# Chunked gated linear attention with experts on one core: level products split by rows per head

## The reference

```python
x = x + layernorm(attn(layernorm(x)));  x = x + layernorm(ffn(layernorm(x)))
# attn, 4 heads, key size 64, value size 128, per batch and head:
q = (x @ Wq) * 64 ** -0.5;  k = x @ Wk;  v = x @ Wv
g = log_sigmoid(x @ gk_w1 @ gk_w2 + gk_b) / 16
for t in range(512):                       # S is 64 x 128
    S = exp(g[t])[:, None] * S + k[t][:, None] * v[t][None, :]
    o[t] = q[t] @ S
o = rms_norm(o) * rms_w * silu(x @ Wg);  out = o @ Wo
# ffn: the 16 x 512 tokens in 8 groups of 1024, one expert each: gelu(t @ w1 + b1) @ w2 + b2
```

## Time and profile before

| | |
|---|---|
| median of 3 runs | 1318.27 us (1318.04 to 1319.22) |
| profiled execution | 1316.67 us |
| its span | 1314.9 us, granted clock 0.988 |
| busy: PE / its weight loads / DVE / ACT / POOL | 95 / 83 / 79 / 54 / 48% of the span |
| instructions | 23430 |
| read from and written to HBM | 28.38 and 8.39 MB |

### The profile page before, as it was taken

How to read it: one execution, slowest core, us unless ns; L and a number is a source line. 1 busy time by engine, 2 the same in 40 slices (tenths; PEclk the granted TensorE clock), 3 DMA queues, 4 the chain that set the end, 5 groups by cost and what they waited for, 6 DMA issues and landing times. The chain is left out here.

```text
span 1314.9 us, 23430 instructions
## 1 busy us (share of the span) xinstructions
PE 1245.6 (95%) x8388; PEld 1096.4 (83%) x8388; DVE 1035.5 (79%) x2404; ACT 711.3 (54%) x1427; POOL 637.5 (48%) x889
## 2 busy tenths in 40 slices
PE   5889999999999999999999999999999999999957
PEld 3778889888898888889888888988889888898956
DVE  4769788796978969788787978879787796978863
ACT  5365555655456465654756555565545646465423
POOL 5436453563445544564435644356354554456431
PEclk9989999999999999999999999999999999999988
DMA  2110010100101001010011001010010100100000
GB/s 97 37 33 17 17 49 1 53 17 17 49 21 48 3 17 49 22 49 2 17 49 53 16 17 47 3 53 16 17 49 18 44 9 17 49 21 33 1 17 16
DMA packets 31778, 38.27 MB, mean 29 GB/s; under 512 B 2448, under 2 KB 29104, under 8 KB 31664
## 3 DMA queue, kind: packets, MB, share of 16 engines
q1 hardware_dynamic: 31136, 36.25, 8.3%
q10 hardware_dynamic: 528, 0.52, 0.1%
HBM read 28.38 MB, written 8.39 MB: 28 GB/s over the span
## 5 line engine op out<-in xcount | busy, mean ns | idle before, releaser
L1041 POOL TENSOR_TENSOR k_decayed<-k_decayed,block_totals 128x256 f32<-128x256 f32 x192 | 170.4, 887 | 248.3 <-PE ps_level L304 248.0
L304 PE MATMUL ps_level<-q_blockdiag,k_decayed 128*128 128x128 f32 x1792 | 263.9, 282 | 13.2 <-DVE q_blockdiag L586 12.5
L304 PEld LDWEIGHTS ps_level<-q_blockdiag,k_decayed 128*128 128x128 f32 x1792 | 234.9, 191 | 34.9 <-DVE q_blockdiag L586 24.6
L576 DVE COPY_PREDICATED attn_T<-level_masks,ps_level 128x512 f32<-128x512 uint32 x160 | 153.1, 957 | 21.6 <-PE ps_level L304 21.4
L1047 POOL TENSOR_TENSOR rstd<-rstd,minus_half 128x1 f32<-128x1 f32 x192 | 111.7, 584 | 106.5 <-DVE rstd L638 106.5
L586 DVE TENSOR_TENSOR q_blockdiag<-q_blockdiag,block_totals 128x512 f32<-128x512 f32 x192 | 140.0, 730 | 27.3 <-PE ps_level L304 27.2
L261 PE MATMUL ps_big<-w_ff_hi,h_hi 128*128 128x256 f32 x512 | 150.0, 293 | 2.5 <-DVE h_lo L591 2.5
L263 PE MATMUL ps_big<-w_ff_hi,h_lo 128*128 128x256 f32 x512 | 144.8, 283 | 0.0
L262 PE MATMUL ps_big<-w_ff_lo,h_hi 128*128 128x256 f32 x512 | 144.7, 283 | 0.0
L838 ACT ACTIVATE gelu_out<-ps_big,ff_b_cols 128x512 f32<-128x512 f32 x128 | 88.0, 688 | 80.2 <-PE ps_big L263 48.9
L624 DVE SCALAR_TENSOR_TENSOR o<-o,o_rstd,out_gate 128x128 f32<-128x128 f32 x256 | 93.3, 425 | 45.0 <-POOL o_rstd L1063 45.0
(11 more groups left out here) (110 smaller groups left out, 3203.1 us busy)
## 6 DMA issues: line engine op xcount, KB each, us to landing
w_raw<-L_ffn_w SPq DMA_DIRECT2D x16, 1024.0 KB, 5.5
out<-y SPq DMA_DIRECT2D x16, 512.0 KB, 2.9
x_in<-L_attn_x SPq DMA_DIRECT2D x15, 512.0 KB, 3.9
ff_b_rows<-L_ffn_b SPq DMA_DIRECT2D x8, 128.0 KB, 2.1
x_in<-L_attn_x ACTq DMA_DIRECT2D x1, 512.0 KB, 4.0
w_raw<-L_attn_Wv SPq DMA_DIRECT2D x1, 512.0 KB, 5.4
w_raw<-L_attn_Wg SPq DMA_DIRECT2D x1, 512.0 KB, 6.7
y<-L_attn_Wo SPq DMA_DIRECT2D x1, 512.0 KB, 7.7
```

The source lines that it names most:

```text
L304: last = nc.tensor.matmul(PL[tl][:, c * CH:(c + 1) * CH], kk[:, tl, c * CH:(c + 1) * CH], q[:, :, :, 1, :], start=True, stop=True)
L576: nc.vector.copy_predicated(dst, m.to_broadcast([P, 2 * NCH, HC // h, h]), src)\
L1041: nc.gpsimd.tensor_tensor(k, k, t.to_broadcast([P, T // (2 * h), h]), ALU.mult)\
```

## The change

- q is stored plainly in `q_decayed` (`qd`), 128 partitions by 512 tokens for each tile, written by DVE straight from PSUM. `q_blocks` on ACT falls. `q_update` handles half the elements, and stands ahead of the copy in DVE's queue.
- `level` takes each head alone: weights and streamed q are on 64 partitions, 64 columns are streamed, and the two heads write to two different banks. Even levels use `ps_out` and `ps_state`, odd ones `PL`, and a bank holds one head of both tiles. In the last level only the first 64 k tokens of a chunk are loaded. A level waits for the copies of the level before the last.
- The copies to attn_T go by head and not by tile, each after both tiles' products, one step later than before.
- `S` becomes block-diagonal, `state_blockdiag`. `state(c)` writes four pieces of 64 partitions; `att` multiplies plain q of a tile by 256 columns of S, two products for a chunk in place of four.
- The own-token products: `diag_rows` streams q times k over a 32-column indicator, chunk c on columns 32c to 32c+31 of the array, ahead of level 0; ACT copies the rows to a spare piece of `o`, and `diag_columns` transposes them.
- The transposes of k for the last chunk, which nothing uses, fall, and the last k update leaves that chunk out.

```diff
 def level(i, tl):
     ...
-                        if i - 1 < MASKED:
-                            pe.wait_ge(sem["dv_cp"], at("dv_cp", s, 2 * (i - 1) + tl + 1))
-                        else:
-                            pe.wait_ge(sem["ac_cp"], at("ac_cp", s, 2 * tl + 2))
+                        if i >= 2:
+                            pe.wait_ge(sem["dv_cp"], at("dv_cp", s, 2 * (i - 1)))
+                        elif C:
+                            pe.wait_ge(sem["dv_t"], at("dv_t", p, NCH))
+                    m = CH if i < NL - 1 else HC
                     for c in range(NCH):
-                        q = qbd[:, tl, :, c * CH:(c + 1) * CH].rearrange("p a (n t h) -> p a n t h", t=2, h=h)
-                        last = nc.tensor.matmul(PL[tl][:, c * CH:(c + 1) * CH],
-                                                kk[:, tl, c * CH:(c + 1) * CH], q[:, :, :, 1, :],
-                                                start=True, stop=True)
-                        if i == 0:
-                            self_product = diag(c, tl)
+                        for hh in range(2):
+                            r = slice(hh * HK, (hh + 1) * HK)
+                            q = qd[r, tl, c * CH:(c + 1) * CH].rearrange("p (n t h) -> p n t h", t=2, h=h)
+                            w = (tl * NCH + c) * HC
+                            last = nc.tensor.matmul(LVB[i % 2][hh][0:m, w:w + HC], kk[r, tl, c * CH:c * CH + m],
+                                                    q[:, :, 1, :], start=True, stop=True)
                     last.then_inc(sem["pe_lv"], 1)
+                def diag_rows():
     ...
+                    for tl in range(KT):
+                        for c in range(NCH):
+                            last = nc.tensor.matmul(PT[0][32 * c:32 * (c + 1), 0:CH], ind[:, tl, :],
+                                                    qk[:, tl, c * CH:(c + 1) * CH], start=(tl == 0), stop=(tl == KT - 1))
+                    last.then_inc(sem["pe_drow"], 1)
+
+                def diag_columns():
+                    pe.wait_ge(sem["ac_dg"], at("ac_dg", s, 1))
     ...
+                    nc.tensor.transpose(PT[1][:, 0:CH], o[:, 0, 0:CH], ident[:, :]).then_inc(sem["pe_diag"], 1)
 def att(c):
     ...
-                        if c:
-                            last = nc.tensor.matmul(PO[:, w], qbd[:, tl, hh, c * CH:(c + 1) * CH],
-                                                    S[:, tl, :], start=False, stop=True)
+                    if c:
+                        for tl in range(KT):
+                            last = nc.tensor.matmul(PO[:, tl * 2 * HV:(tl + 1) * 2 * HV], qd[:, tl, c * CH:(c + 1) * CH],
+                                                    S[:, tl, :], start=False, stop=(tl == KT - 1))
 queue of PE
+                        if step == 0:
+                            diag_rows()
                         level(step // 2, step % 2)
+                        if step == 1:
+                            diag_columns()
 queue of DVE
-                        if step // 2 < MASKED:
-                            copy_pairs(step // 2, step % 2)
                         q_update(step // 2, step % 2)
+                        if step == 1:
     ...
+                        if 1 <= step <= 2 * MASKED:
+                            copy_pairs((step - 1) // 2, (step - 1) % 2)
 def state(c): (DVE)
     ...
+                    for tl in range(KT):
+                        for hh in range(2):
+                            r = slice(hh * HK, (hh + 1) * HK)
+                            new, old = PS[r, tl * HV:(tl + 1) * HV], S[r, tl, hh * HV:(hh + 1) * HV]
     ...
 queue of ACT
-                def q_blocks(tl):
     ...
+                if B:
+                    act.wait_ge(sem["pe_drow"], at("pe_drow", s, 1))
+                    copy(o[:, 0, 0:CH], PT[0][:, 0:CH], "ac_dg")
```

More of the change, by code:

```diff
@@ L64, in build @@
         y = sb("y", [P, NCH, D])
-        qbd = sb("q_blockdiag", [P, KT, 2, T])
+        qd = sb("q_decayed", [P, KT, T])
         kk = sb("k_decayed", [P, KT, T])
@@ L72, in build @@
         kT = sb("k_tokens", [P, NCH, D])
-        S = sb("state", [P, KT, HV])
+        S = sb("state_blockdiag", [P, KT, 2 * HV])
         v = sb("v", [P, NCH, DV])
@@ new lines, in level @@
+                    last.then_inc(sem["pe_lv"], 1)
+                def diag_rows():
+                    if C:
+                        pe.wait_ge(sem["dv_oglo"], at("dv_oglo", p, NCH - 1))
+                    else:
+                        pe.wait_ge(c_ready, 3)
+                    pe.wait_ge(sem["dv_q"], at("dv_q", s, 2 * KT - 1))
+                    for tl in range(KT):
[3 more added lines that the diff above has]
+                    last.then_inc(sem["pe_drow"], 1)
@@ L321, in x3t @@
                     pe.wait_ge(sem["dv_oglo"], at("dv_oglo", p, 3 + kt))
+                    if B and kt:
+                        pe.wait_ge(sem["dv_dg"], at("dv_dg", s, 1))
                     transpose_tokens(xh, kt).then_inc(sem["pe_x3t"], 1)
@@ L355, in kh @@
                         pe.wait_ge(sem["dv_x3lo"], at("dv_x3lo", p, f + 1))
-                    for c in range(2):
+                    for c in range(2 - f):
                         for tl in range(KT):
@@ L450, in att @@
                     for hd in range(H):
-                        tl, hh = hd // 2, hd % 2
                         w = slice(hd * HV, (hd + 1) * HV)
-                        last = nc.tensor.matmul(PO[:, w], Am[:, tl, 2 * c + hh, :], v[:, c, w],
-                                                start=True, stop=(c == 0))
-                        if c:
-                            last = nc.tensor.matmul(PO[:, w], qbd[:, tl, hh, c * CH:(c + 1) * CH],
-                                                    S[:, tl, :], start=False, stop=True)
+                        last = nc.tensor.matmul(PO[:, w], Am[:, hd // 2, 2 * c + hd % 2, :], v[:, c, w],
+                                                start=(hd == 0), stop=(c == 0 and hd == H - 1))
+                    if c:
+                        for tl in range(KT):
+                            last = nc.tensor.matmul(PO[:, tl * 2 * HV:(tl + 1) * 2 * HV], qd[:, tl, c * CH:(c + 1) * CH],
+                                                    S[:, tl, :], start=False, stop=(tl == KT - 1))
                     last.then_inc(sem["pe_att"], 1)
@@ L878, in g_evac @@
                     nc.scalar.activation(gs[:, c, :], PB[1][:, :], ACT.Silu).then_inc(sem["ac_g"], 1)
-                def q_blocks(tl):
-                    act.wait_ge(sem["dv_q"], at("dv_q", n, 2 * tl + 2))
-                    if B:
-                        act.wait_ge(sem["pe_att"], at("pe_att", s, NCH))
-                    else:
-                        act.wait_ge(c_ready, 3)
-                    for hh in range(2):
-                        r = slice(hh * HK, (hh + 1) * HK)
-                        copy(qbd[r, tl, hh, :], qg[r, tl, :], "ac_qb")
                 def og_hi(c):
@@ L902, in run @@
                 for step in range(1, 2 * NL):
-                    if B and step // 2 >= MASKED:
-                        copy_blocks(step // 2, step % 2)
+                    if B and (step - 1) // 2 >= MASKED:
+                        copy_blocks((step - 1) // 2, (step - 1) % 2)
                     if C and 3 <= step < 3 + FT:
@@ L918, in run @@
                         act.wait_ge(sem["pe_kt"], at("pe_kt", s, f + 1))
-                        copy(kT[:, 2 * f:2 * f + 2, :], PT[f][:, :].rearrange("p (c d) -> p c d", c=2), "ac_kt")
+                        copy(kT[:, 2 * f:NCH - 1 if f else 2, :].rearrange("p c d -> p (c d)"), PT[f][:, 0:(2 - f) * D], "ac_kt")
                 if A:
@@ L995, in late_constants @@
             def late_constants():
-                nc.gpsimd.memset(qbd[:, :, :, :], 0.0).then_inc(c_ready, 1)
+                nc.gpsimd.memset(S[:, :, :], 0.0).then_inc(c_ready, 1)
                 fill(masks[:, :, :], 1.0)
-                fill(ind[:, :], QSCALE)
-                select(ind[:, 0:1], [[0, 1]], HK - 1, -1)
-                select(ind[:, 1:2], [[0, 1]], -HK, 1)
+                fill(ind[:, :, :], 0.0)
+                for tl in range(KT):
+                    pool.wait_ge(c_step, count[0])
+                    fill(ind[:, tl, 2 * tl:2 * tl + 2], QSCALE)
+                    select(ind[:, tl, 2 * tl:2 * tl + 1], [[0, 1]], HK - 1, -1)
+                    select(ind[:, tl, 2 * tl + 1:2 * tl + 2], [[0, 1]], -HK, 1)
                 for i in range(MASKED):
```

115 lines of the change are left out of this document (53 added, 62 removed).

## The result

The changed kernel takes 1337.86 us (median; 1335.98 to 1338.32), the kernel before beside it 1318.74 us (1318.04 to 1319.48): ratio 1.0138, 95% interval 1.0125 to 1.0150. It is slower by 1.4%, and the forecast was 1330. The profiled execution has a span of 1336.2 us against 1314.9, 21.3 us more.

A forecast was written before the change was run, and what follows sets the result against it. PE's stream of weight loads and matmuls sets the time. +3.3-0.2-1.1-0.2+0.1-0.3-0.35-0.3, unrounded +0.86 us a batch, times 15 is +13, first batch -1: 1330 us; 8-in-10 range 1262 to 1352.

The forecast's parts named there:

- The pace of the levels: Level products: row halves overlap in pairs, 128-column loads still 0.112 us a round; no gain in 12 of 14 visits.
- Rivals 1 and 3: 1: halves don't overlap, 1516 us, chance 0.12; 3: load on 64 rows takes half the time, 1249 us, 0.08.
- The stay: Levels: one round trip into and out of the split array shape costs 0.33 us; ten a batch, +3.3 us.
- Rival 2: Levels: no drain between whole array and row halves, so the 3.3 us fall; 1270 us, chance 0.12.
- second part of a batch: First feed-forward product to end of levels: stays at 0.33 us each, last level -0.2, h_lo wait -0.3.
- The start of a batch: Before the first feed-forward product: own-token products -1.1 us, stays at 0.33 each, q update and ACT copy waits -0.35.
- rival 4: PE's waits give way: two us more go as DVE and ACT are lighter; 1300 us, chance 0.12.
- att and the state: att's products with the state: +0.1 us a batch; longer state updates on DVE taken as 0, bound +0.5.
- third part: After the levels, with state, att and ogt: k_tokens transposes -0.2 us, att +0.1, out_gate eviction wait -0.3.
- rival 5: DVE's longer state updates and moved copies start a new wait: +1 us a batch, 1345 us, chance 0.09.
- The ends: First batch: shorter q updates, -1 us; last batch priced among the 15 with feed-forward, +0.86 us each.

The follow-up runs named there:

- run 4: Changed kernel with 64 weight columns, not 128, in every level of batches with feed-forward, part of attn_T missing: 1297.88 us, ratio 0.9855.
- run 1: Changed kernel with both tiles of a level together, then two feed-forward pieces: seven stays on the row halves, not twelve; 1309.76 us, ratio 0.9956.
- run 6: Changed kernel with one or two 128-row state updates on DVE, not four of 64, second head's state block left out: 1320.5 us, ratio 1.0043.
- run 7: All edits of the change except the level split and what hangs on plain q; whole-array levels, narrow state: 1306.93 us, ratio 0.9915.
- run 2: Kernel before, whole-array levels, with both tiles of a level together, then two feed-forward pieces: 1325.81 us, ratio 1.0079.
- Run 5: Kernel before with the own-token products by column groups as its only change: 1318.55 us, ratio 1.0018.

## Why the prediction was right, and where its sizes were not

**The pace of the levels: right.** A level is bound by its 128-column loads; loads on different rows overlap in pairs, 0.111 us apart (forecast 0.11), and run 4 halved the columns and got 0.059. The Trainium skill, TensorE: Matmul & The Clock Gate, LDWEIGHTS, says that a load's time goes by its columns and not by its rows, and both distances agree with it. The twofold gain in the Overview of the Trainium skill's TensorEngine Tiling (Array Packing) was not to be had for this shape. Rivals 1 and 3 fall.

**The stay: right.** Forecast 0.33 us, measured 2.63-2.28 = 0.35 a step, and 0.36 from run 1. The Trainium skill, TensorEngine Tiling (Array Packing), Key Properties, agrees: changing the tiling drains TensorE. Rival 2 falls. Steps two parts long: forecast for the second part of a batch 8 x 0.33 - 0.2 - 0.3 = +2.1 us, measured +1.91.

**The start of a batch: right, too small.** Forecast -1.1 + 0.66 - 0.35 = -0.8 us, measured -1.32. The own-token rows took 0.57 us (forecast 0.56), and the wait for ACT's small copy 0.3 (forecast 0.4). The rest is waits that gave way, for q updates first (rival 4's mechanism, half a microsecond of it).

**att and the state: the step that was mis-sized.** I took the four state updates as 0 with a bound of +0.5, because the first of them lies in DVE's wait for o_rstd. The second does not: it stands in DVE's queue ahead of the gates, ogT_lo and og(1). Forecast for the third part -0.2 + 0.1 - 0.3 = -0.4 us; measured +0.27, so 0.67 is missing, and run 6's middle batches are 9.3/14 = 0.66 shorter. Rival 5 had the mechanism, at 1 us. That the middle batch came out at 0.97 us for 0.86 is luck: I had 0.5 us too little for the gain at its start and 0.67 too little for the state, and the two nearly cancel.

**The ends: wrong.** I priced the last batch like the others. There the projections that cover the chain through the state are gone, and of its 5.6 us 5.0 fall behind the levels. PE's products of the second chunk's state, before and after, and the attn_T product behind them in after:

```profile
1250.33 0.66 PE L435 MATMUL ps_state<-v,k_tokens 128*64 128x128 f32 x8 [1.64 <-DVE state L610]
1267.39 0.66 PE L438 MATMUL ps_state<-v,k_tokens 128*64 128x128 f32 x8 [2.46 <-DVE state_blockdiag L624]
1267.98 2.00 PE L455 MATMUL ps_out<-v,attn_T 128*128 128x128 f32 x8
```

The wait for the state is longer at both later chunks, 2.46 us for 1.64 and 2.26 for 0.99. Behind the first of them the granted clock falls, to a mean of 0.68 from 1267.98 to 1278.70, where it is 1.00 in the same stretch before and in run 6. The last product above takes 2.00 us and in run 6 1.16, and the `att` of the second and third chunk together 7.3 us and not 4.1. Run 6, with shorter updates, has neither loss, and its last batch is 6.7 us shorter than in after. No run has one loss without the other, so their shares stay open, and so does whether the longer wait brought the clock down. And I gave the first batch -1 us for shorter q updates; it took 2.1 more, for which the clock is again the likely cause (below).

The forecast of +12 us for the profiled execution falls 9.4 us short of 21.3: 1.6 in the middle, 3.1 at the first batch and 4.7 at the last. The time of 1337.86 us lies as near to rival 5 (1345) as to the forecast (1330); what speaks for the forecast's mechanism is the price of the stays and the pace of the loads, not the total.

## What the runs showed of the hardware

**TensorE's clock in the first batch.** There the levels run one after another with no feed-forward between. Two stretches of after, then the first of them in the kernel before and in run 7 (columns as in the earlier trace rows):

```profile
50.00:57.00 7.00, 6.89 (x64) 6.73 (x64) 4.94 (x8) 0.00 (x0) 2.70 (x3) 0.50 0.02 4
57.00:64.00 7.00, 7.00 (x68) 7.00 (x66) 4.59 (x10) 0.00 (x0) 3.47 (x4) 0.50 0.00 1
```

```profile
50.00:57.00 7.00, 5.61 (x41) 4.70 (x40) 6.88 (x12) 0.00 (x0) 3.92 (x5) 1.00 0.00 0
```

```profile
50.00:57.00 7.00, 5.11 (x36) 4.28 (x36) 7.00 (x11) 0.00 (x0) 3.95 (x5) 1.00 0.01 2
```

After has the 1.2 GHz level (0.50), the others the 2.4 GHz level, though after's PE is busy all but 0.11 us of 14, which is in part the slower clock itself; before it fell, PE ran split levels for some microseconds at 0.97. All kernels here with split levels show 0.50 from 50 to 64 us, stays few or many (run 1 too); before, run 2 and run 7, all on the whole array, show 1.00. Run 5 has whole-array levels and own tokens by column groups, and shows 0.76 from 50 to 57. So in the first batch the split levels go with the low clock, but why stays open. It is the likely cause of most of the first batch's +3.1 against the forecast: run 7's first batch, without it, takes 68.5 us and not 70.6. In the middle batches, with feed-forward between, the clock stayed at 1.00.

**POOL's small power beside DVE's subtraction.** The 4-element step of o_rstd takes 1.01 us in every one of 64 cases before, and in after 1.86 us in 15 of 64, each time while DVE's 1024-element subtraction of two tensors runs over it:

```profile
722.19 1.86 POOL L1072 TENSOR_TENSOR o_rstd<-o_rstd,minus_half 128x4 f32<-128x4 f32 x1
```

The Trainium skill, SBUF — State Buffer, Who interferes with whom, says that a DVE instruction with two inputs in SBUF contends with a GpSimd one that reads SBUF. The trace agrees, within 0.14 us of a step that begins only behind the subtraction: DVE's ends at 721.93+1.25 = 723.18, 1.01 us behind that would be 724.19, and POOL's step ends at 722.19+1.86 = 724.05. It is not what made after slow: DVE then stands idle for o_rstd for only 0.18 us (0.32 before), since its own queue is nearly that long. Run 1 has the same 15 cases.

## What to carry to other kernels

Splitting a product by rows gave nothing here, because its weight loads, and not the streamed columns, set the pace: compare the distance between loads with the columns streamed, and split only with fewer weight columns. Each stay in another shape costs about 0.35 us here, so put all the small products together and alternate their rows; the order of the visits decided whether this change won or lost. An update that a new layout cuts into more, smaller instructions is priced by what stands behind it in its queue, and again for the batch at the end that has no cover.
